# Decoder feed-forward: sum, third norm and fourth norm issued one step later in each round

## The reference, cut to what matters

```python
x_self = _prob_sparse_self_attn(x, self_out_w, self_out_b)     # 16 heads, top-k scores
x = _layernorm(x + x_self, ln1_g, ln1_b)
x_cross = _mha_cross(x, memory, ...)                            # 16 heads, 77 keys
x = _layernorm(x + x_cross, ln2_g, ln2_b)
h = jax.nn.gelu(x @ ffn_w1.T + ffn_b1, approximate=False)
x_ffn = h @ ffn_w2.T + ffn_b2
x = _layernorm(x + x_ffn, ln3_g, ln3_b)
return x
...
x = _layernorm(x + _L1_xattn_ref(x, ctx_1024, ...), axis=-1)
```

## Time and profile before

| | us |
|---|---|
| median of 3 runs | 9407.54 (9402.67 to 9410.44) |
| profiled execution, its own time | 9422.34 |
| its span | 9420.6 |
| decoder stage, from the first round with a feed-forward to the last store (7332.9 to 8929.9) | 1597.0 |
| in that stage, busy: PE, DVE, ACT, POOL | 1172.47, 1037.22, 1009.41, 576.30 |
| in that stage, granted clock of TensorE | 0.85 of full |

### The profile page before, as it was taken

The page is one execution under the profiler, slowest core; times in us unless marked ns, Lnnn a source line. Parts: engine busy times, 40 slices in busy tenths (PEclk is TensorE's granted clock), DMA queues, the critical chain, the costliest instruction groups (busy, mean ns, idle before and its releaser), DMA issues. The chain is left out here.

```text
span 9420.6 us, 94893 instructions
## 1 busy us (share of the span) xinstructions
PE 6652.0 (71%) x26087; PEld 3535.0 (38%) x26087; DVE 6963.6 (74%) x15198; ACT 4421.7 (47%) x8791; POOL 4926.9 (52%) x2845
## 2 busy tenths in 40 slices
PE   5888788887888878887887455455555777777633
PEld 2333333333333333333554333334333545555411
DVE  5999789996999879997554666666666666666466
ACT  3555555554555555554553222222224666666522
POOL 4888688886888868886442333333312333333200
PEclk8888888898888888888888777777756988888755
DMA  4333333333333333332001544444410000000000
GB/s 166 156 134 147 142 137 151 145 155 129 141 156 135 142 148 138 153 142 100 24 25 31 140 127 134 129 127 127 134 47 24 8 12 8 8 8 8 15 17 19
DMA packets 367461, 915.92 MB, mean 97 GB/s; under 512 B 28006, under 2 KB 259930, under 8 KB 298842
## 3 DMA queue, kind: packets, MB, share of 16 engines
q1 hardware_dynamic: 324378, 703.12, 19.8%
q0 software_dynamic: 42880, 210.80, 7.8%
HBM read 870.56 MB, written 56.70 MB: 98 GB/s over the span
## 5 line engine op out<-in xcount | busy, mean ns | idle before, releaser
L376 POOL TENSOR_TENSOR mb_dBu<-mb_dtu,mb_rows_b 128x1024 f32<-128x1024 f32 x1036 | 2423.8, 2357 | 321.1 <-POOLq L63 171.5
L390 DVE TENSOR_TENSOR_SCAN mb_bank<-mb_bank,mb_dBu 128x1024 f32<-128x1024 f32 x704 | 1612.4, 2290 | 90.1 <-PEq L63 90.1
L361 ACT ACTIVATE mb_bank<-mb_dt,mb_a_neg 128x508 f32<-128x508 f32 x2056 | 1314.6, 670 | 0.8
L430 PE MATMUL mb_bank<-mb_hcd,ident 128*128 128x512 f32 x2560 | 1264.6, 621 | 53.5 <-DVE mb_hcd L404 53.5
L430 PE MATMUL mb_bank<-mb_hcp,ident 128*128 128x512 f32 x1280 | 800.7, 759 | 351.8 <-POOL mb_hcp L413 351.8
L1501 POOL DMA_INDIRECT ex_rows<-in_ex_table,ex_idx x536 | 519.5, 969 | 964.1 <-PE ex_bank L1586 705.5
L413 POOL TENSOR_TENSOR mb_hcp<-mb_hs,mb_rows_c 128x1024 f32<-128x1024 f32 x320 | 752.1, 2350 | 367.5 <-DVE mb_hs L390 365.4
L404 DVE TENSOR_TENSOR mb_hcd<-mb_bank,mb_rows_c 128x1024 f32<-128x1024 f32 x704 | 862.1, 1225 | 31.4
L430 PEld LDWEIGHTS mb_bank<-mb_hcd,ident 128*128 128x128 f32 x2560 | 500.7, 202 | 769.3 <-issue 588.8
L390 DVE TENSOR_TENSOR_SCAN mb_hs<-mb_bank,mb_dBu 128x1024 f32<-128x1024 f32 x320 | 730.9, 2284 | 51.7 <-ACT mb_bank L361 51.7
L430 PEld LDWEIGHTS mb_bank<-mb_hcp,ident 128*128 128x128 f32 x1280 | 286.5, 237 | 806.5 <-POOL mb_hcp L413 477.2
(11 more groups left out here) (365 smaller groups left out, 14027.6 us busy)
## 6 DMA issues: line engine op xcount, KB each, us to landing
mb_rows_b<-bc_rows SPq DMA_DIRECT2D x268, 1024.0 KB, 7.9
mb_rows_c<-bc_rows SPq DMA_DIRECT2D x264, 1024.0 KB, 6.9
mb_r_tok<-stream SPq DMA_DIRECT2D x76, 256.0 KB, 2.8
mb_r_post<-stream SPq DMA_DIRECT2D x68, 256.0 KB, 2.9
stream<-mb_r_post SPq DMA_DIRECT2D x68, 256.0 KB, 2.3
ex_rows<-in_ex_table,ex_idx POOLq DMA_INDIRECT x536
bc_rows<-mb_xp SPq DMA_DIRECT2D x68, 64.0 KB, 1.6
ex_x_tok<-stream SPq DMA_DIRECT2D x17, 256.0 KB, 2.9
```

The lines of the kernel that those rows point to most:

```text
L361: e = nc.scalar.activation(da_of(n)[:, c * GB:(c + 1) * GB, 1:], dt[q][:, c].rearrange("p (b t) -> p b t", b=GB)[:, :, 1:], ACT.Exp, scale ...
L376: nc.gpsimd.tensor_tensor(by_c(dBu[m % RING][:]), by_c(chains(dtu[q][:])), over_c(rows_b[:, n]), ALU.mult).then_inc(s["mb_dbu"], 1)
L390: nc.vector.tensor_tensor_scan(flat(to), flat(da_of(n)), flat(dBu[n % RING][:]), 0.0, ALU.mult, ALU.add).then_inc(s["mb_scan"], 1)
L430: m = nc.tensor.matmul(bank[:, B_Y + c], ident[:], part[:, c * GB:(c + 1) * GB], start=False, stop=False)
```

## The change

The chain from the feed-forward's sum on is issued one step later on each engine: the sum and `n3` on DVE from step 9 to 10, `n3` on POOL and ACT from 10 to 11, `b_3` and `x_res` on POOL from 11 to 12, `n4` on DVE from 12 to 13, on POOL from 13 to 14, and its rows on ACT from 14 to 15, the last step. PE's and SP's programs are the same.

```diff
--- before.py
+++ after.py
@@ -2119,9 +2119,9 @@
                         if t == 7 and has_ffn:
                             pool.wait_ge(p["r"], 16)
                             nc.gpsimd.tensor_tensor(x_res[:], x_res[:], wide(rows[:, G1 + 5]), ALU.add).then_inc(p["y3"], 1)
-                        if t == 10 and has_ffn:
+                        if t == 11 and has_ffn:
                             n3.pool(pool)
-                        if t == 11 and has_ffn:
+                        if t == 12 and has_ffn:
                             pool.wait_ge(p["n3_rows"], 1)
                             nc.gpsimd.tensor_tensor(b_3[:], xn3[:], wide(rows[:, G1 + 4]), ALU.mult).then_inc(p["y3"], 1)
                             pool.wait_ge(p["y3"], 2)
@@ -2134,7 +2134,7 @@
                                 at.wait(pool, "pv", 7)
                                 at.wait(pool, "added", 3)
                             pool_next(pool)
-                        if t == 13 and has_ffn:
+                        if t == 14 and has_ffn:
                             n4.pool(pool)
 
                 @block.tensor
@@ -2231,7 +2231,7 @@
                             act_next(act)
                         if t == 13 and has_own:
                             n1.act(act, a1, xn1)
-                        if t == 14 and has_ffn:
+                        if t == 15 and has_ffn:
                             n4.act(act, x_res, y_tok)
 
                 @block.vector
@@ -2247,7 +2247,7 @@
                                                     .to_broadcast([NC, GB, H, DK]), ALU.add).then_inc(p["vb"], 1)
                         if t == 2 and has_ffn:
                             n2.dve_done(dve)
-                        if t == 9 and has_ffn:
+                        if t == 10 and has_ffn:
                             dve.wait_ge(p["f2"], 1)
                             dve.wait_ge(p["bf"], 2)
                             nc.vector.tensor_tensor(a3[:], b_f[:], bank[:, L].rearrange("p (b d) -> p b d", b=GB),
@@ -2257,7 +2257,7 @@
                             n3.dve_done(dve)
                         if t == 10 and has_own:
                             n1.dve_done(dve)
-                        if t == 12 and has_ffn:
+                        if t == 13 and has_ffn:
                             dve.wait_ge(p["y3"], 3)
                             n4.dve_rows(dve, x_res, range(GB))
                             n4.dve_done(dve)
```

## The result

| | before | after |
|---|---|---|
| median of 19 runs | 9407.54 | 9433.27 (9422.82 to 9442.44) |
| ratio, 95% interval | | 1.0024 (1.0017 to 1.0031) |
| profiled execution, its span | 9422.34, 9420.6 | 9435.89, 9434.1 |
| first, last store (L2092) | 7432.51, 8929.95 | 7428.79, 8943.66 |
| granted clock in the decoder stage | 0.85 | 0.83 |

Slower by 25.7 us. The forecast was 9440 (9400 to 9468), slower by more than 0.2%. One of the 19 runs before took 12985.38 us, a slow one that the ratio leaves out. The profiled pair differs by 13.5 only, since the profiled execution of before lies 14.8 above its median and that of after 2.6. Their last stores differ by 13.7: 3.7 are gained ahead of the first store, the twelve store-to-store times of the loop give +17.7, round 14 +3.6, round 15 -3.6, round 16 -0.3.

The account below looks back on a forecast made before the run. No engine is full; a round is a chain through all, ending 4.52 us after `y_tok`. 8 x 3.6 + 5 x 0 + 4.6 = +33.4 on the 9407.5 median gives 9440.9, taken as 9440, range 9400 to 9468.

Parts of the forecast that it names:

- The case that it stands on: Decoder rounds: L805 held by a `km`, low clock gone from its place in most long rounds; 9430 to 9441, chance 0.47.
- The tail, +3.5 of `y_tok` behind L1018: Round's end on ACT: `y_tok` now follows L1018 and is done at 8075.59 against 8072.07, +3.5 us.
- The store's landing and the barrier behind it are these 4.52 us: Round's end on SP: a round ends 4.52 us after `y_tok` is ready, from store to next load.
- nothing hides it: Round's end: the tail's +3.5 us is paid in full, as store and round's end hang on `y_tok`.
- The middle, 0.84 and then 1.75: Mid-round on PE: L975 starts 0.84 us early with `n3` later; `n4` out of step 12 makes the gain 1.75.
- The meeting at 3.4: Step 13 on DVE: `n4`'s L805 meets POOL's running `km` and takes 3.4 us, losing the 1.75 and 0.1 more.
- the second rival: Step 13: L805 is past before `km` starts, 1.75 kept, short rounds +1.75, long -2.9; 9396 to 9411, chance 0.25.
- Long rounds at 0: Loop's long rounds: -1.0 us if the low clock stretch goes, +3.6 if it stays; weighed to -0.1, say 0.
- The four to one: Long rounds: weight given to the low clock stretch going with PE's wait of 2.54 us, against staying or moving.
- the first rival: Decoder rounds: the lower clock stays or moves, all thirteen rounds take 3.6 us more; 9459 and more, chance 0.17.
- Short rounds +3.6: Loop's short rounds: the tail's +3.5 us plus 0.1 left after the meeting takes the middle's 1.75.
- +3.5 - 1.75 + 1.85: Short round: tail +3.5 us, middle's gain 1.75, then the meeting at L805 loses that 1.75 and 0.1 more.

Follow-up runs that it names:

- e1: The changed kernel with only ACT's `n4` rows (`y_tok`) put back to step 14: 9391.02 us, 0.9972 of the kernel before.
- e3: The kernel before, with the store's landing awaited a round later, ahead of the next write of `y_tok`: 0.9999 of the kernel before.
- e2: The kernel before with only ACT's `n4` rows (`y_tok`) moved from step 14 to 15: 9471.85 us, 1.0057 of the kernel before.
- e12: The kernel before with only `n4`'s statistics one step later (DVE 12 to 13, POOL 13 to 14): 1.0009 of the kernel before.
- e5: The changed kernel with 20 more transposes at the end of PE's program in rounds with a feed-forward: 1.0017 of the kernel before.

## Why the prediction was right, and where it was not

The total was right in part by luck. The case that it stands on (L805 meets a `km`, and the lower clock goes from its place in the long rounds) came true in neither half, and the terms below don't add up to the rounds that were measured.

**The tail, +3.5 of `y_tok` behind L1018: right.** From the last `ot` on the chain is as forecast. The rows `y_tok` start 107.57 behind the last store after and 104.15 in e1: 3.42, on a base that agrees within 0.1 at 98 us.

**"The store's landing and the barrier behind it are these 4.52 us", "nothing hides it": wrong.** PE's last instruction ended 3.32 behind the store, at 8075.42, and PE's next began 1.18 later; I had both rows, and took the engine with the named wait for the one that ended the round. The landing had 0.8 of slack, shown by e3 and by the 3.73 that are left when the landing does bound (4.52 - 3.73 = 0.79). The tail's path cost is thus 3.4 - 0.8 = 2.6 and not 3.5. No pair of loops shows 2.6: the mean round is 3.4 longer after than in e1, and 4.8 longer in e2 than before.

**The middle, 0.84 and then 1.75: right along the path.** The waits moved as forecast. From the L975 with the wait of 0.84 to the second one behind it, PE took 10.06 before (8046.93 to 8056.99) and takes 9.16 after (8055.32 to 8064.48): 0.90 for `n3`. For `n4`, e12's short round shows 0.91. In the loop e1's rounds are 1.9 under the mean of before.

**The meeting at 3.4: price right, place wrong.** It was forecast for PE's scores at full clock, by 0.25 us, and in e12's short rounds, where they run at it, the `km` is 0.19 ahead and L805 takes 3.44. In the changed kernel an earlier group of scores runs at the lower clock (L949 2.26, not 1.2). Measured from the store, L805 comes 1.07 later than in e12's short round and the `km` 1.98 later, so that it starts 0.7 behind L805. So the second rival's condition came true, which I had at 0.25, but not its 9396 to 9411: no round came to 104.7 + 1.75.

**Long rounds at 0: right in size, for another reason.** They were 109.2 and are 109.2. The low stretch at 7942.7 to 7956.7 shrank but did not go: 8065.9 to 8069.4 is left of it, and the one behind the border is longer (2.9 to 16.5 behind the store, where it was 9.8 to 16.6 in the round from 7967.43). The four to one I gave for its going was wrong, and the first rival (it stays, 9459) was wrong in adding 3.6 for it.

**Short rounds +3.6: the sum of terms failed, its total held.** There is no sum of +3.5 - 1.75 + 1.85. Every round is at 109.2 (the first at 108.9): the four of 103.1 to 106.4 went there (+5.0, +6.1, +4.6, +2.8 in their order) and the eight long ones stayed. 1.5 on average over twelve is the 17.7. For the last rounds, 14 came at +3.6, the number forecast but not for its reason (the middle alone is +2.2 there, by e1, and the tail on top of it +1.4), 15 at -3.6 and not +1 (e1, without the tail, has -3.4). The forecast for the profiled pair was +22.6, measured 13.5; for the medians +33.4, measured 25.7. That the size came out is luck: the tail's 3.4 happens to be the distance between two of the lengths at which rounds settle.

What stays open is why the kernel before settles at no length, and why just these lengths. In after, the low stretches stand at the same places behind the store in one round as in the next (2.9 to 16.5, then from 26.8, 40.4, 54.1, 71.1 and 91.6), and in before they don't. That they shift until a round repeats is my reading of this and was not tested.

## What to carry to other kernels

Before pricing a shift at a barrier, look for the engine whose last instruction ends latest before it: the one that waits by name may have slack. Where the stretches at the lower clock stay in place, a path's sum held (e12's short round). In a loop whose rounds repeat at one length with such stretches in them, a term of one or two microseconds may cost nothing or a whole step, so forecast the set of lengths, and not the sum. And to get the gain of such a shift, keep the last link off the store: the middle alone, or the whole change with the store left open, is 0.28 or 0.27% faster than before.

## What the runs showed that I had not expected

- Rounds settle at 105.8, 109.2 or 112.6 us: nine of the twelve edited kernels show one of these lengths in every round of the loop but the first, within 0.4 us, through edits that add 1.4 to 2.4 us to an engine.
- The lower clock also stands over work: 0.54 from 8065.9 to 8069.4, PE busy 3.50 of 3.50 us, 1.4 behind the end of an idle time of 1.60.
- Removing it for 6.8 us behind the border (e5, from 9.7 and not 2.9 us behind the store) saved 0.5 to 0.7 on ACT in the first 11 us, and nothing behind it, since PE waits there for DVE's top-k work.
- A TENSOR_SCALAR of 4 elements a partition waits for the end of POOL's `km`: 2.95 and 3.44 us where it takes 0.17 alone.
